# Decoder layer with a routed last stage: engine lists reordered at the step boundaries and in the last step

## The chip, the cores and the metric

The kernel runs on one core of a Trainium2 chip. The metric is the device time of one execution in microseconds, median of the runs shown.

## The reference

Three residual blocks over x of shape (4, 1024, 256), float32, each followed by a layer normalisation:

```python
x = _layernorm(x + gated_conv_scan(x))        # sigmoid gate, 5-tap conv, scan h = a*h + u, W_out, its own layernorm
x = _layernorm(x + slot_gru(x, ctx))          # 3 iterations, per batch: slots = x (1024 rows), context of 64 rows:
    #   attn = softmax over slots of (rmsnorm(slots) @ Wq.T) @ k.T; attn /= sum over context; updates = attn @ v
    #   r, z = sigmoid(...); n = tanh(xn + r * hn); slots = (1 - z) * n + z * slots   (six 256x256 products)
x = _layernorm(x + expert_w[argmax(x @ gate_w.T)] @ x)   # 8 experts, each token goes through one of them
```

## The kernel before, in words

**Stages.** The first block fills the first 113 us. The second takes most of the rest: three iterations over two pairs of batches are six *steps*, k = 0 to 5 (`LAST` = 5). A step is eight *units* (k, q), q = 0 to 7, each 24 matmuls of 128x512 on TensorE (`unit`, L1394): in the order R, HN, XN, Z, each with `hidden` products (six matmuls on the slots, split into `slots_hi` and `slots_lo` for precision) and `update` products (two on `at`, the attention, likewise split). XN is update products alone. The products of a unit land in PSUM banks that the other engines read: ScalarE makes r (`r_gate`), n (`n_gate`) and z (`z_gate`); VectorE makes r*hn (`hidden_part`, L1797), adds xn (`input_part`, L1804), both together being `candidate(k, q)`, and mixes in `settle(k, q)` (`mix`, L1822 and L1824; after every second unit the cast to `slots_hi`, L1829); GpSimd makes slots minus n (`difference`, L1015) and `slots_lo` (L1028).

**Attention between the steps.** While step k runs, the attention of step k+1 is made, since two steps in a row are of different batch pairs: `mean_squares` on TensorE (L1322, fed by `ss_low`, L1755 on VectorE), then `scores` and `sums` (TensorE), exponentials and the `normaliser` on ScalarE (Ln, then Exp), and last on VectorE `attention(k+1)`: the product `sc` (L1779, 128x1024) and, for each half h of the pair, a cast to `at` (L1788) and the difference for its low part (L1790). ScalarE loads a new function table before Ln and before sigmoid or tanh.

**What sets the order.** Each engine runs its own list, written out by hand, and waits on semaphores. There is no scheduler: a call moved in the list of an engine moves the work.

**The last step.** Between the units of step 5 stand 32 *token tiles* (`token_tile`, L1353, 4 matmuls on 128 tokens: gate scores and transposed rows), each followed by `score` (VectorE, L1846) and `row`, `row_square` (ScalarE, L767, L774). Tokens are routed in *groups* of tiles: `choose(g)` and `destinations(g)` on VectorE with `ranks(g)` on TensorE between, `side(g)`, and then GpSimd sends every tile's rows to their place in a buffer in device memory, sorted by expert (`send_row`, L1043, an indirect DMA per tile). Before, there are six groups of 8, 8, 4, 4, 4, 4 tiles. `add_ident` (L1906, VectorE) adds twice the identity to the expert weights once they are loaded; that carries the residual.

**Sorted tiles.** The sorted rows come back through SyncE's queue as 39 tiles (`gather`, three a group, TG = 3). Each goes through `turn` (TensorE transpose, L1454), `copy_turned` (ScalarE, L781), `expert` (TensorE, L1481, 4 matmuls), `statistics` (VectorE, L1982), `variance`, `inverse` (ScalarE), `offset` (VectorE, L2009), `normalise` (ScalarE, L797) and `send_out` (GpSimd, L1051, an indirect DMA). The first `NSOON` = 12 tiles are full and can be worked on when only the first `SOON` = 3 groups (20 token tiles) have been sent: `soon_table` says where they lie. The other `NLAST` = 27 need all groups, and two tables on VectorE, `last_counts` and `last_places`, and SyncE waits for them (`base_set`).

```python
for g in range(SOON):
    sp.wait_ge(row_out[g], 16 * GROUPS[g][1])     # L488
...
for g, (t0, n) in enumerate(GROUPS):              # L1122
    for t in range(t0, t0 + n):
        send_row(t, g)
```

## Time and profile before

| | us |
|---|---|
| median of 3 runs | 638.34 (637.24 to 638.39) |
| the profiled execution | 638.83 |
| its span in the profile | 637.1 |
| TensorE busy | 546.8 (86%) |
| VectorE busy | 457.4 (72%) |
| ScalarE busy | 373.3 (59%) |
| GpSimd busy | 253.5 (40%) |
| mean granted TensorE clock | 0.922 |

The span is the time between the first and the last instruction; the run time adds 1.7 us around it. Busy times are of one core, and the engines overlap. All starts below are in microseconds from the span's start. A matmul row's end is modelled, so rows of TensorE can overlap by a little.

### The profile page before, as it was taken

How to read it: one execution, taken by the hardware profiler on the slowest of the kernel's cores; microseconds unless marked ns; L12 is line 12 of the kernel's file. 1: busy time of each engine (PE TensorE's matmuls, PEld its weight loads, DVE VectorE, ACT ScalarE, POOL GpSimd, SP SyncE). 2: the span in 40 equal slices, each digit the busy share in tenths (PEclk: the TensorE clock that was granted, in tenths of full speed). 3: DMA queues.
4: the chain of work that ended last, by engine and by line, in shares of the span. 5: the costliest groups of instructions: out<-in, count | busy, mean ns of one | idle time of the engine just before them, and what ended most of it. 6: DMA issues, size and time to landing. Idle time of an engine off the chain costs nothing.

```text
span 637.1 us, 7357 instructions
## 1 busy us (share of the span) xinstructions
PE 546.8 (86%) x2158; PEld 402.8 (63%) x2158; DVE 457.4 (72%) x806; ACT 373.3 (59%) x661; POOL 253.5 (40%) x239
## 2 busy tenths in 40 slices
PE   6999897597799979997997999799989886858781
PEld 3474536265578857876785788578878764636560
DVE  3999899985894995799489758964756579653431
ACT  4558195865665846584666668475756544634542
POOL 1032302021042564456454744543443462554453
PEclk9999897679899989998999999899999997878776
DMA  8921003010110000000000000020110724145421
GB/s 296 329 82 66 1 0 132 0 68 0 67 66 1 1 1 1 1 0 1 1 0 1 1 1 1 1 66 24 42 51 26 254 102 125 69 127 141 121 77 34
DMA packets 23896, 37.88 MB, mean 59 GB/s; under 512 B 3246, under 2 KB 15663, under 8 KB 23601
## 3 DMA queue, kind: packets, MB, share of 16 engines
q1 hardware_dynamic: 20448, 28.98, 14.5%
q0 software_dynamic: 3408, 8.43, 3.7%
q8 instruction: 18, 0.29, 0.2%
q14 instruction: 22, 0.17, 0.1%
HBM read 23.60 MB, written 14.72 MB: 60 GB/s over the span
## 4 chain that ended last, share of the span: by engine, by line
PE 46%; DVE 19%; issue 10%; ACT 8%; another core or an unknown queue 1%; POOL 0%; ACTq 0%; DVEq 0%; POOLq 0%
PE psum L1409 25%; PE psum L1481 7%; PE psum L1334 4%; DVE slots_full L1824 2%; DVE gru L1822 2%; DVE gru L1797 2%; PE psum L1454 2%; DVE at L1788 2%; PE psum L1158 2%; DVE sc L1779 2%; PE psum L1379 2%; DVE at L1790 2%; DVE ss_part L1755 1%; PE psum L1228 1%; PE psum L1247 1%
## 5 line engine op out<-in xcount | busy, mean ns | idle before, releaser
L1409 PE MATMUL psum<-slots_hi,w_hh 128*128 128x512 f32 x576 | 189.3, 411 | 15.3 <-DVE gru L1797 12.0
L1409 PEld LDWEIGHTS psum<-slots_hi,w_hh 128*128 128x128 f32 x576 | 109.4, 194 | 42.8 <-DVE gru L1797 13.7
L1015 POOL TENSOR_TENSOR gru<-slots_full,gru 128x512 f32<-128x512 f32 x43 | 67.8, 1576 | 161.7 <-ACT gru L744 161.6
L1409 PE MATMUL psum<-slots_lo,w_hh 128*128 128x512 f32 x288 | 116.7, 405 | 0.0
L1409 PE MATMUL psum<-at,v_ih_pair 128*128 128x512 f32 x288 | 92.9, 404 | 2.1 <-DVE at L1790 2.1
L1797 DVE SCALAR_TENSOR_TENSOR gru<-psum,vec,gru 128x512 f32<-128x512 f32 x48 | 35.9, 748 | 46.7 <-PE psum L1409 40.1
L1481 PE MATMUL psum<-slots_full,w_tile 128*128 x156 | 54.2, 482 | 14.7 <-issue 8.5
L1409 PEld LDWEIGHTS psum<-at,v_ih_pair 128*128 128x128 f32 x288 | 54.8, 193 | 17.1 <-DVE at L1790 3.9
L744 ACT ACTIVATE gru<-gru,vec 128x512 f32<-128x512 f32 x48 | 34.7, 723 | 52.3 <-DVE gru L1804 51.5
L1409 PEld LDWEIGHTS psum<-slots_lo,w_hh 128*128 128x128 f32 x288 | 55.8, 194 | 13.4
L1145 PE MATMUL psum<-early_hi,w_in 128*128 128x512 f32 x128 | 57.6, 608 | 5.1 <-DMA early_hi<-in_xT 4.9
L1028 POOL TENSOR_TENSOR slots_lo<-slots_full,slots_hi 128x512 fp32r<-128x512 f32 x32 | 52.3, 1634 | 0.6 <-DVE slots_hi L1829 0.6
L1051 POOL DMA_INDIRECT out<-out_tile,out_index x39 | 38.2, 979 | 34.1 <-ACT out_tile L797 23.6
L738 ACT ACTIVATE gru<-psum,brz 128x512 f32<-128x512 f32 x48 | 32.8, 682 | 30.4 <-PE psum L1409 29.7
L1481 PEld LDWEIGHTS psum<-slots_full,w_tile 128*128 128x128 f32 x156 | 33.6, 238 | 24.8 <-issue 20.5
L1043 POOL DMA_INDIRECT sorted_rows<-row_block,dest x32 | 32.9, 1028 | 36.8 <-DVE dest L1882 24.9
L1145 PEld LDWEIGHTS psum<-early_hi,w_in 128*128 128x128 f32 x128 | 24.7, 195 | 35.6 <-issue 33.8
L1824 DVE TENSOR_TENSOR slots_full<-gru 128x512 f32<-128x512 f32 x48 | 38.1, 795 | 1.7
L1982 DVE BATCH_NORM_STATS2 st<-psum 128x6 f32<-128x256 f32 x39 | 16.7, 428 | 28.8 <-PE psum L1481 19.1
L781 ACT ACTIVATE w_tile<-psum 128x256 f32<-128x256 f32 x39 | 14.9, 384 | 37.6 <-PE psum L1454 20.6
L1822 DVE TENSOR_TENSOR gru<-gru 128x512 f32<-128x512 f32 x48 | 35.2, 733 | 0.2
L751 ACT ACTIVATE gru<-psum,brz 128x512 f32<-128x512 f32 x48 | 32.7, 682 | 4.1 <-PE psum L1409 3.1
(250 smaller groups left out, 1015.3 us busy)
## 6 DMA issues: line engine op xcount, KB each, us to landing
gathered<-sorted_rows SPq DMA_DIRECT2D x39, 129.0 KB, 1.9
x_scratch<-slots_full SPq DMA_DIRECT2D x8, 512.0 KB, 3.0
x_block<-x_scratch SPq DMA_DIRECT2D x8, 512.0 KB
early_hi<-in_xT SPq DMA_DIRECT2D x3, 1024.0 KB, 5.7
x_tm<-in_x SPq DMA_DIRECT2D x4, 512.0 KB, 6.9
slots_full<-in_expertT SPq DMA_DIRECT2D x1, 2048.0 KB, 11.1
sorted_rows<-gru SPq DMA_DIRECT2D x1, 1032.0 KB, 12.1
early_hi<-in_xT SPq DMA_DIRECT2D x2, 512.0 KB, 4.3
```

What stands on the lines that cost most here:

```text
L738: act.activation(X(u), psum[:, R_B + u % 2, :], ACT.Sigmoid, bias=brz[:, c, 0:1]).then_inc(r_act, 1)
L744: act.activation(X(u), X(u), ACT.Tanh, bias=col(c, V_BIH + 2)).then_inc(n_act, 1)
L1015: pool.tensor_tensor(DF(u), full[:, c, seq(k, h), blk(j)], X(u), ALU.subtract).then_inc(d_pool, 1)
L1028: last = pool.tensor_tensor(slots[1][:, c, b, blk(j)], full[:, c, b, blk(j)], slots[0][:, c, b, blk(j)].bitcast(F32), ALU.subtract)
L1043: pool.indirect_dma_start(rows[:], bass.IndirectOffsetOnAxis(dest[:, n:n + 1], 0), rowb[:, row_slot(n), :], None, bounds_check=E * REGION - 1,
L1051: pool.indirect_dma_start(out[:], bass.IndirectOffsetOnAxis(oidx[:, g % 4, t:t + 1], 0), og[:, i % (4 * TG), :], None, bounds_check=TOK - ...
L1145: last = pe.matmul(psum[:, bank + j, :], wi[:, k, at_col:at_col + P], xF[b % 2][:, k, cols_of(j)], start=k == 0, stop=k == C - 1)
L1409: last = pe.matmul(psum[:, bank, :], w, d, start=start and i == 0, stop=stop and i == len(pairs) - 1)
L1481: last = pe.matmul(expert_out(i), wT[:, i % TG, c, :], ew[:, c, bass.ds(off, D)], start=c == 0, stop=c == C - 1)
L1797: dve.scalar_tensor_tensor(out=X(u), in0=psum[:, HN_B, :], scalar=col(c, V_BHH + 2), in1=X(u), op0=ALU.add, op1=ALU.mult).then_inc(t_dve, 1)
L1822: dve.tensor_tensor(Z(u), Z(u), DF(u), ALU.mult).then_inc(e_dve, 1)
L1824: dve.tensor_tensor(full[:, c, seq(k, h), blk(j)], X(u), Z(u), ALU.add).then_inc(s_dve, 1)
```

## The change

1. **Between steps, VectorE.** `attention` keeps its product; the two halves' cast and difference become `spread_attention(f, h)`. Before: `candidate(k, 6)`, `settle(k, 5)`, product, both halves, `candidate(k, 7)`, `settle(k, 6)`. Now: `candidate(k, 6)`, product, half 0, `settle(k, 5)`, `candidate(k, 7)`, `settle(k, 6)`, half 1.
2. **ScalarE tables.** After the Exp of `rms` and of `normaliser` the table for sigmoid and tanh is named at once, so that nine loads fall away (46 to 37 in its list).
3. **Last step, TensorE.** Token tiles come about three sooner (tiles 0 and 1 already inside unit (4, 7)), and there are five groups, of 8, 8, 8, 4, 4 tiles. `ranks(0)` to `ranks(2)` stand inside units 2, 4 and 5, `ranks(3)` after unit 7, and tiles 28 to 31 between the first turns instead of behind the third expert product.
4. **15 sorted tiles ahead of the rest.** `NSOON` is 15 and `NLAST` 24; since group 2 has 8 tiles, 24 token tiles have to be sent before the first gather. `last_counts` moves before `offset(0)` and `last_places` before `offset(1)` on VectorE.
5. **`add_ident` goes to GpSimd** (a 128x1024 addition each), ahead of the row sends of group 2 and of group 3; `mean_f` is rewritten to twice the identity for it.
6. **Smaller ones.** The last `add_block` on VectorE is split in two halves; `out_index` waits for `turn_ev`; the last group of three sorted tiles is finished as two and one; the waits for the output DMAs at the end go from GpSimd to SyncE; gathers of tiles 12 to 14 wait for turned tiles.

```diff
-        GROUPS = ((0, NT), (NT, NT), (2 * NT, TJ), (2 * NT + TJ, TJ), (3 * NT, TJ), (3 * NT + TJ, TJ))
+        GROUPS = ((0, NT), (NT, NT), (2 * NT, NT), (3 * NT, TJ), (3 * NT + TJ, TJ))
...
-        NSOON = 4 * TG
+        NSOON = 5 * TG
...
                     act.activation(inv[:], inv[:], ACT.Exp, scale=-1.0).then_inc(d_rd, 1)
+                    act.preload_act_table_set("sigmoid_and_others")
...
+                def add_ident(c):
+                    pool.wait_ge(ew_in, 16)
+                    part_c = ew[:, c].rearrange("p (e d) -> p e d", d=D)[:, :, c * P:(c + 1) * P]
+                    eye = mean_f[:].rearrange("p (a n) -> p a n", a=1).broadcast_to([P, E, P])
+                    pool.wait_ge(two_set, 1)
+                    pool.tensor_tensor(part_c, part_c, eye, ALU.add).then_inc(ew_id, 1)
...
                 for g, (t0, n) in enumerate(GROUPS):
+                    if g == 2:
+                        add_ident(0)
+                    if g == 3:
+                        add_ident(1)
                     for t in range(t0, t0 + n):
                         send_row(t, g)
...
                     candidate(k, 6)
+                    attention(k + 1)
+                    spread_attention(k + 1, 0)
                     settle(k, 5)
-                    attention(k + 1)
+                    if not later:
+                        gate_centre()
                     candidate(k, 7)
-                    settle(k, 6)
+                    if later:
+                        settle(k, 6)
+                    spread_attention(k + 1, 1)
```

VectorE's list at the end of a step, before, from the cast that ends `settle(k, 5)` on (L1779 the product, L1788 and L1790 a half's cast and difference, L1797 and L1804 `candidate(k, 7)`, L1822 and L1824 `settle(k, 6)`, L1755 `ss_low`):

```order
L1829 CAST slots_hi<-slots_full 128x2x512
L1779 SCALAR_TENSOR_TENSOR sc<-sc,small,inv 128x1024
L1788 CAST at<-sc 64x1024
L1790 TENSOR_TENSOR at<-sc,at 64x1024
L1788 CAST at<-sc 64x1024
L1790 TENSOR_TENSOR at<-sc,at 64x1024
L1797 SCALAR_TENSOR_TENSOR gru<-psum,vec,gru 128x512
L1804 TENSOR_TENSOR gru<-psum,gru 128x512
L1822 TENSOR_TENSOR gru<-gru 128x512
L1824 TENSOR_TENSOR slots_full<-gru 128x512
L1755 TENSOR_TENSOR ss_part<-ss_block,ss_part 128x512
```

And now, from the cast of the first half on (L1822 is now a half's cast and L1824 its difference, L1856, L1858 and L1863 are `settle`, L1831 and L1838 `candidate(k, 7)`, L1788 `ss_low`):

```order
L1822 CAST at<-sc 64x1024
L1824 TENSOR_TENSOR at<-sc,at 64x1024
L1856 TENSOR_TENSOR gru<-gru 128x512
L1858 TENSOR_TENSOR slots_full<-gru 128x512
L1863 CAST slots_hi<-slots_full 128x2x512
L1831 SCALAR_TENSOR_TENSOR gru<-psum,vec,gru 128x512
L1838 TENSOR_TENSOR gru<-psum,gru 128x512
L1856 TENSOR_TENSOR gru<-gru 128x512
L1858 TENSOR_TENSOR slots_full<-gru 128x512
L1822 CAST at<-sc 64x1024
L1824 TENSOR_TENSOR at<-sc,at 64x1024
L1788 TENSOR_TENSOR ss_part<-ss_block,ss_part 128x512
```

The product and the first half have moved ahead of `settle(k, 5)`, the second half behind `settle(k, 6)`; the set of operations is the same.

TensorE's list before, from the last token tile that stands in the last step (`hot`, `cum` are `ranks(3)`, `gathered` a turn, `w_tile` an expert product):

```order
L1379 MATMUL psum<-eye_and_gate,slots_full 128x137 x2
L1391 MATMUL psum<-hot_1,tri 128x32
L1392 MATMUL psum<-cum_1,ones_f 128x32
L1454 MATMUL psum<-ident,gathered 128x128 x4
L1479 TENSOR_LOAD soon_off
L1479 ISA x2
L1481 ISA
L1481 MATMUL psum<-slots_full,w_tile 128x256
L1481 ISA
L1481 MATMUL psum<-slots_full,w_tile 128x256
```

And now, from `ranks(3)` on:

```order
L1416 MATMUL psum<-hot_1,tri 128x32
L1417 MATMUL psum<-cum_1,ones_f 128x32
L1482 MATMUL psum<-ident,gathered 128x128 x2
L1401 MATMUL psum<-eye_and_gate,slots_full 128x137 x4
L1482 MATMUL psum<-ident,gathered 128x128 x2
L1401 MATMUL psum<-eye_and_gate,slots_full 128x137 x4
L1506 TENSOR_LOAD soon_off
L1506 ISA x2
L1508 ISA
L1508 MATMUL psum<-slots_full,w_tile 128x256
L1508 ISA
L1508 MATMUL psum<-slots_full,w_tile 128x256
```

Tiles 28 to 31 have come in among the first two turns.

GpSimd's list before, from the last `difference` calls (L1015) and `add_x1` (L1037) to the sends:

```order
L1037 TENSOR_TENSOR slots_full<-slots_full,x_block 128x2x512
L1015 TENSOR_TENSOR gru<-slots_full,gru 128x512 x2
L1037 TENSOR_TENSOR slots_full<-slots_full,x_block 128x2x512
L1015 TENSOR_TENSOR gru<-slots_full,gru 128x512
L1037 TENSOR_TENSOR slots_full<-slots_full,x_block 128x2x512
L1015 TENSOR_TENSOR gru<-slots_full,gru 128x512 x2
L1043 DMA sorted_rows<-row_block,dest 33920x258 x32
L1051 DMA out<-out_tile,out_index 4096x256 x39
```

And now (L1031 `difference`, L1053 `add_x1`, L1143 the rewriting of `mean_f`, L1061 `add_ident`):

```order
L1053 TENSOR_TENSOR slots_full<-slots_full,x_block 128x2x512
L1031 TENSOR_TENSOR gru<-slots_full,gru 128x512 x2
L1053 TENSOR_TENSOR slots_full<-slots_full,x_block 128x2x512 x2
L1143 TENSOR_SCALAR mean_f<-ident 128x128
L1031 TENSOR_TENSOR gru<-slots_full,gru 128x512 x3
L1066 DMA sorted_rows<-row_block,dest 33920x258 x16
L1061 TENSOR_TENSOR slots_full<-slots_full,mean_f 128x8x128
L1066 DMA sorted_rows<-row_block,dest 33920x258 x8
L1061 TENSOR_TENSOR slots_full<-slots_full,mean_f 128x8x128
L1066 DMA sorted_rows<-row_block,dest 33920x258 x8
L1074 DMA out<-out_tile,out_index 4096x256 x39
```

The two additions stand ahead of the sends of group 2 and of group 3, in the queue that also issues the DMAs.

## Rows read from the trace of the kernel before

**Rows 1.** The page: the chain that ended last, its share of the span by engine.

```profile
PE 46%; DVE 19%; issue 10%; ACT 8%; another core or an unknown queue 1%; POOL 0%; ACTq 0%; DVEq 0%; POOLq 0%
```

**Rows 2.** Windows (start:end, length, busy per engine, granted clock, DMA share, GB/s), step 3.

```profile
304.30:331.40 27.10, 27.09 (x116) 21.90 (x117) 15.82 (x22) 19.12 (x22) 10.29 (x8) 1.00 0.00 1
331.40:363.30 31.90, 28.40 (x114) 21.89 (x113) 30.46 (x30) 19.11 (x25) 20.65 (x14) 0.95 0.00 1
```

**Rows 3.** TensorE's waits, 200 to 480 us (total, times, longest).

```profile
PE psum L1409 <- DVE gru L1797: 12.0, 4, 3.0
PE psum L1409 <- DVE at L1790: 2.1, 4, 0.9
```

**Rows 4.** TensorE in order of time (start, us) at the boundary 2 to 3.

```profile
349.74 1.22 PE L1409 MATMUL psum<-slots_hi,w_hh 128*128 128x512 f32 x2 [3.00 <-DVE gru L1797]
...
363.29 0.73 PE L1322 MATMUL psum<-ss_part,mean_half 128*128 128x512 f32 x2
```

**Rows 5.** VectorE in order of time at the same boundary.

```profile
340.68 2.31 DVE L1779 SCALAR_TENSOR_TENSOR sc<-sc,small,inv 128x1024 f32<-128x1024 f32 x1
...
343.75 2.20 DVE L1790 TENSOR_TENSOR at<-sc,at 64x1024 fp32r<-64x1024 f32 x1
...
348.93 0.75 DVE L1797 SCALAR_TENSOR_TENSOR gru<-psum,vec,gru 128x512 f32<-128x512 f32 x1
...
361.45 1.78 DVE L1755 TENSOR_TENSOR ss_part<-ss_block,ss_part 128x512 fp32r<-128x512 f32 x1
```

**Rows 6.** VectorE at the boundary 4 to 5, the same operations.

```profile
457.18 1.28 DVE L1779 SCALAR_TENSOR_TENSOR sc<-sc,small,inv 128x1024 f32<-128x1024 f32 x1
...
459.22 1.22 DVE L1790 TENSOR_TENSOR at<-sc,at 64x1024 fp32r<-64x1024 f32 x1
```

**Rows 7.** ScalarE at the boundary 2 to 3.

```profile
340.33 1.28 ACT L751 ACT_TABLE_LOAD   x1
...
342.21 1.04 ACT L759 ACTIVATE sq_block<-slots_full 128x1024 f32<-128x1024 f32 x1
343.16 0.68 ACT L738 ACTIVATE gru<-psum,brz 128x512 f32<-128x512 f32 x1
```

**Rows 8.** TensorE in the last part, from the first sorted tile.

```profile
534.65 0.67 PE L1454 MATMUL psum<-ident,gathered 128*128 128x128 f32 x2
...
538.74 2.07 PE L1481 MATMUL psum<-slots_full,w_tile 128*128 x4 [2.26 <-issue]
...
544.95 2.21 PE L1379 MATMUL psum<-eye_and_gate,slots_full 128*128 128x137 f32 x16
...
549.12 0.39 PE L1390 MATMUL psum<-cum,ones_f 128*128 128x8 f32 x2 [0.50 <-DVE hot L1864]
...
565.85 0.69 PE L1454 MATMUL psum<-ident,gathered 128*128 128x128 f32 x2 [3.65 <-issue]
566.71 3.77 PE L1481 MATMUL psum<-slots_full,w_tile 128*128 x8 [0.17 <-issue]
...
574.60 1.73 PE L1481 MATMUL psum<-slots_full,w_tile 128*128 x4 [3.27 <-issue]
...
579.91 1.13 PE L1481 MATMUL psum<-slots_full,w_tile 128*128 x4
```

**Rows 9.** GpSimd: row sends in order of time; its 128x1024 addition by line.

```profile
507.82 0.97 POOL L1043 DMA_INDIRECT sorted_rows<-row_block,dest  x1 [6.61 <-DVE dest L1882]
...
556.39 0.98 POOL L1043 DMA_INDIRECT sorted_rows<-row_block,dest  x1 [0.30 <-issue]
...
L1037 POOL TENSOR_TENSOR slots_full<-slots_full,x_block 128x1024 f32<-128x1024 f32 x4 | 9.6, 2395 | 0.0
```

**Rows 10.** SyncE's queue: its waits, 520 to 640 us.

```profile
SPq L488 <- DMA sorted_rows<-row_block,dest: 1.9, 1, 1.9
```

**Rows 11.** VectorE: first and last instruction of the two tables (24 in all).

```profile
555.39 0.16 DVE L1944 TENSOR_SCALAR gru<-soon_first 128x8 f32<-128x8 f32 x1
...
561.52 0.24 DVE L1978 TENSOR_SCALAR gru<-gru,i_col 128x27 int32<-128x27 f32 x1
```

More of the change, by code:

```diff
@@ L2133, in _ @@
+                score(26)
+                hidden_part(LAST, 7)
+                score(27)
+                input_part(LAST, 7)
+                choose(3)
+                settle(LAST, 7)
+                add_half(1)
+                destinations(3)
                 side(3)
-                destinations(3)
-                score(26)
-                score(27)
+                for n in range(28, 32):
+                    score(n)
                 choose(4)
-                settle(LAST, 7)
-                add_block(7)
+                statistics(0)
```

396 lines of the change are left out of this document (211 added, 185 removed).

## Prediction

> **What bounds the kernel now.** I read the chain of waits first: TensorE carries 46% of it, VectorE 19% [rows 1]. So neither engine bounds all of the time, and the question is where they change places. I then cut one step (59 us) into two windows [rows 2]. From 304.30 to 331.40 TensorE is busy 27.09 of 27.10 us, and VectorE 15.82: TensorE bounds. From 331.40 to 363.30, around the boundary to the next step, TensorE is busy 28.40 of 31.90 us and VectorE 30.46: there VectorE bounds, with 1.4 us of idle time in 32. TensorE's waits in the steps say the same: four waits for `hidden_part` (L1797) make 12.0 us, 3.0 at each boundary, and four for the low half of the attention make 2.1 [rows 3]. In order of time, TensorE stands 3.00 us until 349.74, because VectorE first finishes product, halves and their casts (from 340.68) and comes to `hidden_part` of unit 7 at 348.93 [rows 4, 5]. The window's last matmul, the mean squares at 363.29, starts when VectorE's `ss_low` ends (361.45 + 1.78 = 363.23) [rows 4, 5]: VectorE's list, not TensorE's, sets when the boundary is over.
>
> In the last part sorted tiles go one after another through all engines. What to see in [rows 8]: the first expert product starts at 538.74, the twelve early tiles end at 566.71 + 3.77 = 570.48, with 3.65 us of waiting before the turn at 565.85; then comes a gap up to 574.60, where the first late tile starts.
>
> **The change, part by part.**
>
> *The boundaries 0-1 to 3-4 (four).* In the new order the product can begin at about 338.8, right behind `candidate(k, 6)`, since it no longer waits for `settle(k, 5)` (some 1.9 us ahead of 340.68, which are `mix` and the cast). Uncontended it takes 1.28 [rows 6] (2.31 in [rows 5]); half 0 follows with a cast and 1.22 to 2.20 [rows 5, 6] and is done by about 343, where TensorE wants it at about 345.5: the wait of 2.1 / 4 = 0.5 goes. `settle(k, 5)` then ends at about 345.2. Here a new wait comes. ScalarE's squares need that settle, and `r_gate` of unit 7 stands behind them: before it ran at 343.16 [rows 7]; now squares (1.04) and gate (0.68) follow the settled slots of about 344.4, which gives 346.1, and VectorE idles some 0.95 us. `hidden_part` of unit 7 ends at about 346.9 instead of 349.7, so TensorE's wait of 3.0 becomes about 1.0. That looks like 2.5 us a boundary. But the operations on VectorE are the same, only in another order, and the next unit's `hidden_part` now stands behind half 1 (about 1.9 us): it ends about where it did, TensorE runs into it, and `ss_low` is as late as before. Over the window VectorE can give back only its idle 1.4 us [rows 2] and what it loses to operations that take longer beside GpSimd's (1.03 for the product, 0.98 for a difference [rows 5, 6], and one cast, not shown, of about the same size): 3.0 together. Against it stand the new idle 0.95 and, at worst, contention for the operations that were free of it. **I take 0 for each**, as nearest to the balance of VectorE's busy time (30.46 of 31.90), with bounds of -3 and +2 us: -12 and +8 for four.
>
> *Table loads.* Nine loads of 1.28 us fall away (the row at 340.33 is one [rows 7]), 11.5 us of ScalarE time. ScalarE waits on VectorE and TensorE around every one of them; `z_gate` comes 1.3 us sooner and its result is wanted later. Value 0; its cover is VectorE's queue, and were that gone, each boundary's load would be worth at most 1.3.
>
> *Boundary 4-5.* Tiles 0 and 1 inside unit (4, 7) wait for `gate_centre`, tile 2 for score and row of tile 0. These waits replace one of the same size. Three tiles more are done when step 5's unit 1 starts, so I carry about 0.65 us of delay, which is hidden behind the next term.
>
> *Up to the first sorted tile.* What decides there is GpSimd's queue: 24 tiles are sent before the first gather, where it was 20. Group 1 began at 507.82 [rows 9], and since `ranks(1)` comes inside unit 4, I put it 2.2 us sooner, at 505.6. A send costs 1.28 us in a row (0.97 and 0.30 between). Then: 8 sends 10.2, `add_ident(0)` 2.4 (the 128x1024 addition by its row [rows 9]), 8 sends 10.2, landing and reading the place about 3.0 (SyncE's wait for it was 1.9 [rows 10]), gather and turn 2.5: 533.9, against 534.65 [rows 8]. With tiles 28 and 29 in the gap behind it I put the first expert product at 537.5 against 538.74: **-1.2**.
>
> *Early tiles.* Before, twelve took 570.48 - 538.74 = 31.7 us. Out of this go tiles 28 to 31 (2.2, the row at 544.95), the ranks of the sixth group (from 549.12, three pairs of small matmuls, some 0.9) and the wait of 3.65, whose chain runs over the tables on VectorE (555.39 to 561.8 [rows 11]): they delayed statistics of tiles 6 to 8, and now stand two groups of tiles sooner, where TensorE goes slower anyway. In come about 1.0 us of waiting, since `offset(0)` and `offset(1)` stand behind the tables. 31.7 - 2.2 - 0.9 - 3.65 + 1.0 = 26.0: the twelfth ends at 563.5. Tiles 12 to 14 follow at the pace of the late ones, (579.91 - 574.60) / 3 = 1.77 [rows 8], until 568.8; the gap at the switch stays (574.60 - 570.48 = 4.1): the first late tile, number 15, at 572.9. Before, it ran at 579.91. **-7.0**. Bounds: -1 (the tables stop the early tiles for their full 6.4 us) and -11 (the gap goes too, since the last send, which ended at 557.4 [rows 9], will end near 549).
>
> *The end.* The last tiles go out as fast as GpSimd issues them, and the split of the last group changes only when the first two are ready: 0. Moving the final waits from one queue to another: 0.
>
> Sum: 638.8 (the profiled execution) - 7.0 = 631.8. That execution is 0.5 us above the median of 638.34, so against the median **631.3**, with the likeliest case's own range of 627 to 635.5.
>
> **Rivals.**
>
> *B, the boundaries gain too.* If the pieces of attention fall where GpSimd is idle, three contended operations a boundary become free: 4 x 3.0 = 12 us more, 619.3. For it: the product begins at 338.8, before GpSimd has the `difference` of unit 6 to do, and VectorE is the bound. Against it: GpSimd's operations start when VectorE's and ScalarE's results come, so they move along.
>
> *C, the additions on GpSimd cost their full time.* They stand between sends that are on the way to the first turn and to the last send, 2.4 us each [rows 9]; if VectorE's routing operations, which read two operands from SBUF, wait for them too, `destinations(3)` and `destinations(4)` are late by as much: 2 x 2.4 = 4.8 off the gain, 636.1. For it: the product on VectorE took 2.31 instead of 1.28 us beside an operation of GpSimd [rows 5, 6]. The Trainium skill, "SBUF — State Buffer", section "Who interferes with whom", says that a VectorE instruction with two SBUF inputs and a GpSimd instruction that reads SBUF lock each other out of a shared port for the whole instruction; it speaks against this part of the change. By that rule the loser would stand still for up to a whole operation, and the trace agrees in direction, with 1.03 us lost where GpSimd's operations take 1.5 or more. Against C: GpSimd stands idle before the sends of group 3, so the second addition may cost nothing.
>
> *D, slower: the new wait of VectorE at each boundary.* Its place is `r_gate(k, 7)` behind the squares. VectorE idles 0.95 us, and where the product falls together with `difference` all the same and one more operation does, 1.03 more are lost; TensorE is behind VectorE for the rest of the window, so both are paid in full: 4 x 2.0 = 8 us, with 0.65 at the last boundary, against the gain of 7.0: 640.0. It decides from 1.7 us a boundary on. For it: 30.46 of 31.90 us busy. Against it: in three of the five operations contention is there already, and it can only move.
>
> *E, nothing.* The sorted tiles are bound by another thing than I think and all gains are waited away: 638.3.
>
> **Chances.** My forecast 0.50, B 0.18, C 0.15, D 0.13, E 0.04. A measurement of this kernel can tell 0.2% (1.3 us) from no change. A, B and C lie below 637.1; a part of C and of A's tail reaches into the band. Faster 0.80, same 0.07, slower 0.13. The range takes in B and most of D: 619 to 640.
>
> **What would show it right or wrong.** Right: at each boundary TensorE's wait of 3.0 splits into two shorter ones, behind `hidden_part` of unit 7 and of the next step's unit 0, and the step stays at 59.0 us; the first turn stands within 1 us of 533.9; no wait over 2 us in front of turn 11; the first late tile at about 573. Wrong: steps of 56 us (B), or of 61 (D, with `r_gate` as what VectorE waits for); a first turn after 536 with GpSimd's additions ahead of it (C); or a wait of 3 us or more behind `last_counts` or `last_places`, which would mean that the tables' price was set too low.

## The result, and the profile after

| | before | after |
|---|---|---|
| median, us | 637.79 (636.31 to 638.39, 4 runs) | 644.64 (644.07 to 644.92, 4 runs) |
| ratio | | 1.011, 95% interval 1.0089 to 1.013 |
| span of the profiled execution | 637.1 | 643.1 |
| mean granted TensorE clock | 0.922 | 0.939 |

The change makes the kernel slower by 1.1%, 6.9 us. The prediction, 631.3 with a range of 619 to 640, is wrong in its sign.

The same places in both traces say where the time went. "Unit (k, q)" is the start of VectorE's `hidden_part` (L1797 before, L1831 now).

| start of | before, us | after, us | difference |
|---|---|---|---|
| the last mean squares of step 1 | 245.30 | 245.14 | -0.2 |
| the same, step 2 | 304.31 | 307.12 | +2.8 |
| the same, step 3 | 363.29 | 369.12 | +5.8 |
| the same, step 4 | 423.27 | 431.11 | +7.8 |
| unit (4, 7) | 463.44 | 472.19 | +8.8 |
| unit (5, 0) | 468.62 | 483.79 | +15.2 |
| unit (5, 7) | 528.94 | 545.09 | +16.2 |
| first expert product | 538.74 | 555.34 | +16.6 |
| sorted tile 15 | 579.91 | 590.37 | +10.5 |
| last expert product | 621.86 | 629.21 | +7.4 |
| end of the span | 637.1 | 643.1 | +6.0 |

So three things happened: the boundaries between steps cost about 9 us up to unit (4, 7), the boundary 4-5 another 6.4 (three more token tiles stand in it, 1.4 us of matmuls at the pace of 0.47 a tile), and the last part, from the first expert product on, gave 10.6 back. Step 5 between them adds 1.4.

The page after, its engines and its chain:

```profile
PE 545.1 (85%) x2154; PEld 401.1 (62%) x2154; DVE 460.6 (72%) x795; ACT 360.6 (56%) x654; POOL 254.6 (40%) x242
...
PE 39%; DVE 23%; issue 12%; ACT 10%; another core or an unknown queue 1%; POOL 0%; POOLq 0%; DVEq 0%; ACTq 0%
```

VectorE carries 23% of the chain where it had 19% [rows 1], ScalarE 10% where it had 8%, TensorE 39% where it had 46%.

**A step.** The window of one whole step, between the same matmuls (columns as in [rows 2]):

```profile
307.10:369.10 62.00, 57.06 (x228) 44.90 (x228) 47.54 (x51) 35.23 (x44) 29.31 (x20) 0.94 0.00 1
```

62.0 us for 228 matmuls, where before it was 27.1 + 31.9 = 59.0. TensorE's waits in the steps, as in [rows 3]:

```profile
PE psum L1434 <- DVE gru L1831: 11.5, 8, 2.0
PE psum L1349 <- DVE ss_part L1788: 10.3, 4, 3.7
```

The four waits of 3.0 us behind `hidden_part` have become eight of 11.5 us in all, the half's wait (2.1) is gone, and four have come, 10.3 us in all, before the last mean squares of each step (L1349), where VectorE's `ss_low` (`ss_part`) is late. Before, there was one such wait in this stretch, of 1.3 us. In order of time at the boundary 2-3, as in [rows 4]:

```profile
351.19 0.73 PE L1434 MATMUL psum<-slots_hi,w_hh 128*128 128x512 f32 x2 [0.74 <-DVE gru L1831]
...
359.05 1.01 PE L1434 MATMUL psum<-slots_hi,w_hh 128*128 128x512 f32 x2 [1.99 <-DVE gru L1831]
...
369.12 0.87 PE L1349 MATMUL psum<-ss_part,mean_half 128*128 128x512 f32 x2 [2.21 <-DVE ss_part L1788]
```

The prediction had the first wait at 1.0 (it is 0.74) and one at unit 0 of the next step (1.99). It had not carried on to the third, 2.21 at the mean squares. VectorE at the same boundary, as in [rows 5]:

```profile
343.00 1.27 DVE L1812 SCALAR_TENSOR_TENSOR sc<-sc,small,inv 128x1024 f32<-128x1024 f32 x1
...
345.03 2.20 DVE L1824 TENSOR_TENSOR at<-sc,at 64x1024 fp32r<-64x1024 f32 x1
...
350.38 0.75 DVE L1831 SCALAR_TENSOR_TENSOR gru<-psum,vec,gru 128x512 f32<-128x512 f32 x1 [0.97 <-ACT gru L752]
...
351.78 1.16 DVE L1856 TENSOR_TENSOR gru<-gru 128x512 f32<-128x512 f32 x1
352.97 1.67 DVE L1858 TENSOR_TENSOR slots_full<-gru 128x512 f32<-128x512 f32 x1
354.67 1.68 DVE L1822 CAST at<-sc 64x1024 fp32r<-64x1024 f32 x1
...
358.25 0.74 DVE L1831 SCALAR_TENSOR_TENSOR gru<-psum,vec,gru 128x512 f32<-128x512 f32 x1
...
364.14 1.56 DVE L1856 TENSOR_TENSOR gru<-gru 128x512 f32<-128x512 f32 x1
365.73 1.67 DVE L1858 TENSOR_TENSOR slots_full<-gru 128x512 f32<-128x512 f32 x1
367.32 1.75 DVE L1788 TENSOR_TENSOR ss_part<-ss_block,ss_part 128x512 fp32r<-128x512 f32 x1
```

What to see here: the product takes 1.27 instead of 2.31, as hoped. The new idle time before `hidden_part` of unit 7 is 0.97, behind ScalarE's `r_gate`. But the difference of half 0 still takes 2.20; then `mix` of unit 6 takes 1.16 and 1.67, where both halves of it took 0.7 before, the cast of half 1 takes 1.68 (1.66 before), and `mix` of unit (3, 1) 1.56 and 1.67. All of them ran beside an operation of GpSimd. Before, the same two `mix` operations of unit 6 were these:

```profile
350.32 0.68 DVE L1822 TENSOR_TENSOR gru<-gru 128x512 f32<-128x512 f32 x1
351.04 0.69 DVE L1824 TENSOR_TENSOR slots_full<-gru 128x512 f32<-128x512 f32 x1
```

From the end of `candidate(2, 6)` to the end of the last `ss_low`, VectorE took 24.5 us (338.71 to 363.23) and takes 26.0 (343.08 to 369.07). Off it went 1.0 for the product, 1.1 for one of the two `ss_low` additions (1.77 before, 0.69 now) and an idle time of 0.8 ahead of unit (3, 1); onto it came 3.2 for `mix` and the new idle 0.97. ScalarE's two lines say why `r_gate` was late:

```profile
348.71 1.06 ACT L773 ACTIVATE sq_block<-slots_full 128x1024 f32<-128x1024 f32 x1 [3.46 <-DVE slots_full L1858]
349.68 0.67 ACT L752 ACTIVATE gru<-psum,brz 128x512 f32<-128x512 f32 x1
```

The squares wait for the settled slots (to 348.71, where [rows 7] had them at 342.21), and `r_gate` of unit 7 follows at 349.68.

The whole run says the same of VectorE by line (columns: name, shapes, count, busy us, mean ns, idle before it). Before, the two operations of `mix` and the product:

```profile
L1824 DVE TENSOR_TENSOR slots_full<-gru 128x512 f32<-128x512 f32 x48 | 38.1, 795 | 1.7
...
L1822 DVE TENSOR_TENSOR gru<-gru 128x512 f32<-128x512 f32 x48 | 35.2, 733 | 0.2
...
L1779 DVE SCALAR_TENSOR_TENSOR sc<-sc,small,inv 128x1024 f32<-128x1024 f32 x5 | 10.5, 2107 | 0.0
```

And after:

```profile
L1858 DVE TENSOR_TENSOR slots_full<-gru 128x512 f32<-128x512 f32 x48 | 47.0, 978 | 1.6
L1856 DVE TENSOR_TENSOR gru<-gru 128x512 f32<-128x512 f32 x48 | 42.1, 876 | 2.9 <-ACT gru L765 2.2
...
L1812 DVE SCALAR_TENSOR_TENSOR sc<-sc,small,inv 128x1024 f32<-128x1024 f32 x5 | 6.4, 1277 | 1.3 <-ACT inv L744 1.3
```

`mix` has grown from 73.3 to 89.1 us with the same 96 instructions; the product has shrunk from 10.5 to 6.4. The `ss_low` additions fell by 4.4 and the casts of the halves by 0.9, so VectorE works 6.4 us longer for the same work. In these lines the reorder put more on some operations than it took off others.

### The profile page after: what moved, and what is told of

Its sections match the earlier page's. It is cut to its first block, busy times and chain, and to the rows that moved or that the text cites. A ratio compares the mean times of both kernels' runs of the same rounds, so it can differ in the third digit from the quotient of the medians.

```text
span 643.1 us, 7343 instructions
## 1 busy us (share of the span) xinstructions
PE 545.1 (85%) x2154; PEld 401.1 (62%) x2154; DVE 460.6 (72%) x795; ACT 360.6 (56%) x654; POOL 254.6 (40%) x242
## 4 chain that ended last, share of the span: by engine, by line
PE 39%; DVE 23%; issue 12%; ACT 10%; another core or an unknown queue 1%; POOL 0%; POOLq 0%; DVEq 0%; ACTq 0%
PE psum L1434 19%; PE psum L1508 5%; DVE slots_full L1858 5%; DVE gru L1856 4%; PE psum L1361 3%; DVE gru L1831 2%; PE psum L1401 2%; DVE ss_part L1788 2%; DVE at L1822 2%; ACT gru L752 2%; PE psum L1185 2%; PE psum L1482 1%; ACT out_tile L814 1%; PE psum L1255 1%
## 5 line engine op out<-in xcount | busy, mean ns | idle before, releaser
L1434 PE MATMUL psum<-slots_hi,w_hh 128*128 128x512 f32 x576 | 191.2, 414 | 14.8 <-DVE gru L1831 11.5
L1434 PEld LDWEIGHTS psum<-slots_hi,w_hh 128*128 128x128 f32 x576 | 110.1, 196 | 44.2 <-DVE gru L1831 15.2
L1031 POOL TENSOR_TENSOR gru<-slots_full,gru 128x512 f32<-128x512 f32 x43 | 66.4, 1544 | 175.8 <-ACT gru L758 175.4
L1831 DVE SCALAR_TENSOR_TENSOR gru<-psum,vec,gru 128x512 f32<-128x512 f32 x48 | 35.9, 748 | 49.5 <-PE psum L1434 37.9
L1508 PE MATMUL psum<-slots_full,w_tile 128*128 x156 | 49.2, 444 | 13.4 <-ACT w_tile L795 8.0
L752 ACT ACTIVATE gru<-psum,brz 128x512 f32<-128x512 f32 x48 | 32.7, 681 | 44.3 <-PE psum L1434 42.2
L1044 POOL TENSOR_TENSOR slots_lo<-slots_full,slots_hi 128x512 fp32r<-128x512 f32 x32 | 48.4, 1512 | 0.6 <-DVE slots_hi L1863 0.6
L1858 DVE TENSOR_TENSOR slots_full<-gru 128x512 f32<-128x512 f32 x48 | 47.0, 978 | 1.6
L1172 PEld LDWEIGHTS psum<-early_hi,w_in 128*128 128x128 f32 x128 | 25.2, 199 | 36.7 <-issue 35.4
L1508 PEld LDWEIGHTS psum<-slots_full,w_tile 128*128 128x128 f32 x156 | 30.5, 217 | 22.9 <-issue 19.5
L1856 DVE TENSOR_TENSOR gru<-gru 128x512 f32<-128x512 f32 x48 | 42.1, 876 | 2.9 <-ACT gru L765 2.2
L1838 DVE TENSOR_TENSOR gru<-psum,gru 128x512 f32<-128x512 f32 x48 | 33.2, 692 | 1.8
L1038 POOL TENSOR_TENSOR ss_block<-sq_block 128x512 f32<-128x512 f32 x16 | 22.2, 1386 | 29.5 <-ACT sq_block L773 29.4
## 6 DMA issues: line engine op xcount, KB each, us to landing
sorted_rows<-gru SPq DMA_DIRECT2D x1, 1032.0 KB, 11.5
```

What stands on the lines that cost most here:

```text
L752: act.activation(X(u), psum[:, R_B + u % 2, :], ACT.Sigmoid, bias=brz[:, c, 0:1]).then_inc(r_act, 1)
L1031: pool.tensor_tensor(DF(u), full[:, c, seq(k, h), blk(j)], X(u), ALU.subtract).then_inc(d_pool, 1)
L1044: last = pool.tensor_tensor(slots[1][:, c, b, blk(j)], full[:, c, b, blk(j)], slots[0][:, c, b, blk(j)].bitcast(F32), ALU.subtract)
L1172: last = pe.matmul(psum[:, bank + j, :], wi[:, k, at_col:at_col + P], xF[b % 2][:, k, cols_of(j)], start=k == 0, stop=k == C - 1)
L1434: last = pe.matmul(psum[:, bank, :], w, d, start=start and i == 0, stop=stop and i == len(pairs) - 1)
L1508: last = pe.matmul(expert_out(i), wT[:, i % TG, c, :], ew[:, c, bass.ds(off, D)], start=c == 0, stop=c == C - 1)
```

## The experiments

The runs came in four series (e1 to e4; r1, r2, e5, e6; e7 to e10; x1 to x4), and the kernel before takes 620.5 us in the first two and about 638 in the others and in the first result: in its two traces (first result and r2) the starts agree within 1 us up to 465 us, and the last part is what differs. So every figure is read within its own series, against the kernel before in that series.

| run | median, us | before in its series | ratio, 95% interval |
|---|---|---|---|
| e1, old boundaries in the changed kernel | 622.99 | 620.67 | 1.0031 (1.0015 to 1.0048) |
| e2, new boundaries alone | 631.47 | 620.67 | 1.0186 (1.0169 to 1.0203) |
| e3, half 1 later | 616.31 | 620.67 | 0.9937 (0.992 to 0.9954) |
| e4, changed, no early tables | 633.12 | 620.67 | 1.0205 (1.0188 to 1.0222) |
| r1, changed again | 632.31 | 620.36 | 1.0183 (1.0151 to 1.0215) |
| r2, before again, one run | 622.76 | 620.36 | |
| e5, e1 and score(1) sooner | 620.54 | 620.36 | 0.9985 (0.9964 to 1.0006) |
| e6, e1 with 12 ahead | 622.14 | 620.36 | 1.0034 (1.0016 to 1.0052) |
| e7, gate ahead of squares | 641.4 | 637.89 | 1.0091 (1.0046 to 1.0135) |
| e8, early tables alone | 637.49 | 637.89 | 0.9999 (0.9978 to 1.002) |
| e9, e5 and identity on VectorE | 634.26 | 637.89 | 0.9939 (0.9918 to 0.9961) |
| e10, half 1 later and score(1) sooner | 631.39 | 637.89 | 0.9875 (0.9827 to 0.9922) |
| x1, changed, third time | 646.87 | 638.54 | 1.0156 (1.0089 to 1.0222) |
| x2, as e9 | 633.42 | 638.54 | 0.9947 (0.991 to 0.9984) |
| x3, as e5 | 632.92 | 638.54 | 0.993 (0.9901 to 0.9959) |
| x4, e10 and row(2) later | 628.28 | 638.54 | 0.9868 (0.9805 to 0.9932) |

**e1: the old boundaries in the changed kernel.**

```diff
                     candidate(k, 6)
+                    if later:
+                        settle(k, 5)
                     attention(k + 1)
                     spread_attention(k + 1, 0)
-                    settle(k, 5)
-                    if not later:
+                    if later:
+                        spread_attention(k + 1, 1)
+                    else:
+                        settle(k, 5)
                         gate_centre()
                     candidate(k, 7)
                     if later:
                         settle(k, 6)
-                    spread_attention(k + 1, 1)
+                    else:
+                        spread_attention(k + 1, 1)
```

`later` is true at the boundaries 1-2 to 3-4; the boundary 0-1 is written out ahead of the loop and has the same edit.

> The changed kernel with VectorE's list put back at the four boundaries 0-1 to 3-4 (settle, product, both halves, then candidate 7); all else as changed, and at the boundary 4-5 the settle only moves ahead of the product. Theory 1 (the reordered list costs about 2.6 us at each boundary through the idle time before hidden_part of unit 7 and more operations that run beside GpSimd's): 644.6 - 4 x 2.1 to 2.6 = 634 to 636. Theory 2 (the boundaries are neutral as forecast, and the loss sits in the last step: more tiles early, additions on GpSimd): 643 to 645.

The edit leaves the boundary 4-5 as it is in the changed kernel: there `settle(4, 5)` stays behind the product and half 0. What the expectation says of that boundary is wrong.

Measured: 622.99, and the changed kernel stood at 632.31 in the next series (r1) and, without its early tables, at 633.12 in this one. So the four boundaries are worth 9 to 10 us. The expectation's absolute numbers went by a before of 637.8; its difference of 8.4 to 10.4 holds.

**e2: the new boundaries alone, in the kernel before.**

```diff
                     candidate(k, 6)
+                    if later:
+                        attention(k + 1)
+                        spread_attention(k + 1, 0)
                     settle(k, 5)
-                    attention(k + 1)
+                    if not later:
+                        attention(k + 1)
+                        spread_attention(k + 1, 0)
+                        spread_attention(k + 1, 1)
                     candidate(k, 7)
                     settle(k, 6)
+                    if later:
+                        spread_attention(k + 1, 1)
```

> The kernel before with only the new order of VectorE's list at the boundaries 0-1 to 3-4. Theory 1: 637.8 + 8 to 10 = 646 to 648, with 61 to 62 us a step and a wait of TensorE for ss_part of about 2 us in each step. Theory 2: 637 to 639.

Measured: 631.47 against 620.67, +10.8 us, a little over the 8 to 10 expected. The window of a step:

```profile
306.90:368.90 62.00, 57.08 (x228) 44.91 (x228) 47.52 (x51) 38.01 (x46) 29.32 (x20) 0.94 0.00 1
```

62.0 us, VectorE busy 47.52, TensorE 57.08 at a granted clock of 0.94: the changed kernel's window within 0.02 us, though ScalarE still has its table loads (38.01 us here, 35.23 there). Theory 1 holds, from both sides, and the forecast of a neutral boundary falls.

**e3: half 1 later.** If VectorE's list bounds the boundary, work must be taken out of it, not turned round in it. TensorE wants half 1 only in unit 4 of the next step.

```diff
                     settle(k, 1)
+                    spread_attention(k, 1)
+                    dve.wait_ge(at_lo, 2 * k + 2)
                     tops(k + 1)
...
                     attention(k + 1)
+                    spread_attention(k + 1, 0)
+                    if not later:
+                        spread_attention(k + 1, 1)
                     candidate(k, 7)
```

As in e2, `attention` is first cut down to the product, so that the halves can be placed by themselves.

> The kernel before, with the second half of the attention (cast and difference) taken out of the boundary and put behind settle(k, 1) of the next step, where VectorE idles; TensorE needs that half only in unit 4. Theory 1 (VectorE's list bounds the boundary): each of four boundaries gives back 2 to 3 us: 626 to 630. Rival (TensorE or the chain through ScalarE bounds it): 636 to 639.

Measured: 616.31, 4.4 us under before: clear of the noise, and about half of the least expected (8 us). Its trace stands further ahead: the last mean squares of step 4 start at 414.23, 9.0 us before those of the kernel before. That trace is of the fastest of its four runs (614.54). One step of it and TensorE's waits:

```profile
298.70:355.70 57.00, 53.99 (x229) 42.64 (x229) 48.02 (x51) 37.87 (x46) 30.74 (x20) 1.00 0.00 1
```

```profile
PE psum L1322 <- DVE ss_part L1755: 10.3, 4, 2.6
```

57.0 us for this step and for the one before it, 58.6 for the one behind it; the waits for `hidden_part` are gone, and what is late next is the `ss_low` in front of the last mean squares, 2.6 us each. That is the wait that the new kernel has too.

**e4 and e8: the early tables, taken out and put in alone.**

```diff
                     act.activation(inv[:], inv[:], ACT.Exp, scale=-0.5).then_inc(rstd_done, 1)
-                    act.preload_act_table_set("sigmoid_and_others")
...
                     act.activation(inv[:], inv[:], ACT.Exp, scale=-1.0).then_inc(d_rd, 1)
-                    act.preload_act_table_set("sigmoid_and_others")
```

This is e4, in the changed kernel; e8 puts the same two lines into the kernel before.

> The changed kernel without the two early table loads, so that the nine loads before sigmoid come back (11.5 us of ScalarE time). If ScalarE is off the path: within 1 us of 644.6. Rival (z_gate of unit 6 and the normaliser's neighbours are on the path): 647 to 650.

> The kernel before with only the early table loads (nine loads fewer). Forecast: no change, within 1 us of the kernel before. Rival (z_gate of unit 6 comes 1.3 us sooner, so that squares, slots_lo and r_gate do, and operations fall apart otherwise): 1 to 4 us faster, or slower where more of VectorE's operations then meet GpSimd's.

Measured: e4 1.0205 of before, the changed kernel in the next series 1.0183, intervals that overlap; e8 0.9999 (0.9978 to 1.002). Taking 11.5 us of work from ScalarE changes nothing that can be measured (e8's interval is 0.2% to either side, 1.3 us).

**r1, r2 and x1: the two kernels again.**

> The changed kernel unaltered, so that the others of this series have it beside them on the same chip. If the four boundaries cost 10 us, as the first series says, and the early tables nothing: within 1 us of the kernel without early tables, 632 to 634, where the kernel before has 620.7. If the early tables were worth something: 630 or less.

> The kernel before unaltered, for its profile on this chip: the same starts up to about 470 us, and a last part that is shorter by about 15 us than in the first profile (620.7 against 637.8 us).

> The changed kernel unaltered on the chip of this series. 1.1 to 1.8% above the kernel before (its two ratios so far: 1.011 and 1.018).

Measured: the changed kernel is slower each time, by 1.1%, 1.8% and 1.6%. r2 took 622.76 in its one timed run, with a span of 621.0. In it the last part runs so (first expert product, first late tile):

```profile
536.23 2.07 PE L1481 MATMUL psum<-slots_full,w_tile 128*128 x4 [2.56 <-issue]
...
568.54 1.81 PE L1481 MATMUL psum<-slots_full,w_tile 128*128 x4 [4.01 <-ACT w_tile L781]
```

32.3 us between them and 52.5 from there to the end, where the first profile of before had 35.9 and 62.5 [rows 8].

**e5: score(1) sooner.** At the boundary 4-5 ScalarE of the changed kernel stands as follows (`row(1)`, then `z_gate` of unit (4, 7), then `r_gate` of unit (5, 0)):

```profile
480.22 0.47 ACT L781 ACTIVATE row_block<-psum,token_scores 128x256 f32<-128x256 f32 x1 [3.90 <-DVE token_scores L1880]
480.59 0.68 ACT L765 ACTIVATE gru<-psum,brz 128x512 f32<-128x512 f32 x1
...
483.08 0.67 ACT L752 ACTIVATE gru<-psum,brz 128x512 f32<-128x512 f32 x1
```

`row(1)` waits 3.90 us for a score, and both gates stand behind it. The score itself stood on VectorE behind `settle(4, 6)`, whose two operations took 1.55 and 2.75 beside two of GpSimd.

```diff
                         score(0)
+                        score(1)
                         settle(k, 6)
...
-                score(1)
                 score(2)
```

> The changed kernel with the old boundaries (as in e1_old_boundaries, 623.0), and score(1) moved on VectorE from behind settle(4, 6) to ahead of it. Theory (at the boundary 4-5 ScalarE has row(1) in front of z_gate of unit 7, and row(1) waits for a score that stands behind two long operations): r_gate of unit (5, 0) comes 3 to 4 us sooner, 619 to 621. Rival (GpSimd's sends or the extra tiles set the last step's end): 622 to 624.

Measured: 0.9985 of before, against 1.0031 for e1: 2.8 us for one moved reduction of 0.2 us. The traces have 1.9 of it at its place: `hidden_part` of unit (5, 0) follows that of (4, 7) by 9.7 us, where it is 11.6 in e1 and in the changed kernel, and 5.2 in the kernel before.

**e6: twelve tiles ahead.** `NSOON = 4 * TG` in e1.

> The changed kernel with the old boundaries and 12 sorted tiles ahead of the last ranks instead of 15 (27 late ones). Theory (three more early tiles move the gap at the switch to a later, then shorter, place): 1 to 3 us slower than 623.0. Rival (the gap waits for the last sends in both cases): the same within 0.5.

Measured: 1.0034 against 1.0031. The rival holds: the wait at the first late tile is there with both counts, and as long (3.77 here, 3.96 in e1):

```profile
568.17 1.13 PE L1508 MATMUL psum<-slots_full,w_tile 128*128 x4 [3.77 <-ACT w_tile L795]
```

So the fifteen sorted tiles, by themselves, gain nothing in these two series.

**e7: the gate ahead of the squares.**

```diff
                     z_gate(k, 6)
+                    r_gate(k, 7)
                     if later:
                         squares(k, 2)
-                    r_gate(k, 7)
```

> The changed kernel with ScalarE's r_gate of unit 7 put ahead of the squares at the boundaries 0-1 to 3-4, so that hidden_part no longer waits for it. It tells the idle time from the contention. If the idle 0.97 us is a loss of its own: 4 us faster than the changed kernel (which is 11.8 us above the kernel before on this chip), thus 7 to 9 us above before. If VectorE's contended operations only take the place of the idle time: 10.5 to 12 above before.

Measured: 1.0091 (1.0046 to 1.0135), 3.5 us over the kernel before, where 7 to 9 was expected if the idle time is a loss of its own. The changed kernel was not run in this series, and the interval is too wide to part 4 us from 1. The traces say more. From the matmuls with `mean_half` on `res` inside step 0 (L1247 of the kernel before, at 187.50) to unit (4, 6) the kernel before takes 266.9 us, the changed kernel 276.9 and e7 272.8. But of the 4.1 us between the last two, 3.1 are two stretches behind the last mean squares that ran at the full granted clock in e7 (35.05 and 35.10 us, where the changed kernel has 36.62 and 36.61), and one such stretch also ran at the full clock in the unaltered changed kernel (r1, 35.08). The four boundaries proper got 1.0 us shorter in all, though four idle times of 0.97 at the gate are gone. So in these traces `r_gate` behind the squares itself costs about 1 us; that the clock held because of its move is not shown. Two boundaries of e7 in order of time:

```profile
304.52 0.74 PE L1349 MATMUL psum<-ss_part,mean_half 128*128 128x512 f32 x2 [0.93 <-DVE ss_part L1788]
...
354.66 0.73 PE L1434 MATMUL psum<-slots_hi,w_hh 128*128 128x512 f32 x2 [2.73 <-DVE gru L1831]
...
364.72 0.73 PE L1349 MATMUL psum<-ss_part,mean_half 128*128 128x512 f32 x2 [2.19 <-DVE ss_part L1788]
```

The wait at unit 7 becomes one of 2.73 at unit 0 of the next step, and the wait at the mean squares is there again, 2.19 at the second of these boundaries and 0.93 at the first.

**e9 and x2: the identity on VectorE.** The two additions go back to VectorE, behind `add_block(6)` and behind the first `add_half`, in e5.

> e5_score_1_sooner with the two additions of the identity back on VectorE (1.21 us each), behind add_block(6) and behind the first half of the last add_block. If GpSimd's additions hold sends or VectorE (rival C): 1 to 4 us faster than e5 (which was 0.2 us above before). If they are hidden there: 0 to 2 us slower, since VectorE has 2.4 us more in the last step.

> As e9_identity_on_vector, now beside x3 on the same chip. If GpSimd's additions cost the last step: 1 to 4 us under x3. If they are hidden: 0 to 2 us above x3.

> As e5_score_1_sooner. Its difference to x1 is four boundaries (10 us by e1) and the score (2.5 us by e5): 11 to 13 us under x1, thus 2 to 4 us under the kernel before where that stands 8 to 10 under x1.

Measured: e9 0.9939, where e5 had 0.9985 in another series; that looked like the 1 to 4 us of rival C. But beside each other in one series x2 takes 633.42 and x3 632.92, no difference. GpSimd's additions (2.4 us each) are hidden, and rival C falls. x3 is 14.0 us under the changed kernel beside it (11 to 13 was expected) and 5.6 under the kernel before (2 to 4 expected): without the reordered boundaries and with one score moved, the rest of the change is a gain (0.993, 0.9901 to 0.9959). In the series of e5 that gain was not to be told from nothing.

**e10 and x4: what beats both.** e10 is the changed kernel with the boundaries as in e3 and the score as in e5. x4 also puts `row(2)` behind `r_gate(LAST, 0)` on ScalarE.

> The changed kernel with three edits: at the four boundaries the old order, but the second half of the attention put behind settle(k, 1) of the next step (as in e3_half_1_later, which gained 4.4 us on before), and score(1) sooner (as in e5, at before's time). If the two gains add up: 4 to 8 us under before. Rival (the last step's end is set by GpSimd's sends, so that an earlier start is waited away): within 2 us of before.

> e10_all_but_reorder with row(2) and its square behind r_gate(5, 0) on ScalarE instead of ahead. In the trace of e5 ScalarE waited 1.97 us for the score of tile 2 there, with r_gate, and VectorE's hidden_part, behind it. If that delay reaches the end of the last step: 1 to 2.5 us under e10 (0.9875 of the kernel before), 0.984 to 0.986. Rival (the tiles' rows bound the last step again): 0.987 to 0.989.

Measured: 0.9875 and 0.9868, the second just above the 0.984 to 0.986 that was expected; 628.28 against 638.54 for before and 646.87 for the changed kernel in the same series. What `row(2)` did: ScalarE in x3 (row 2), and then in x4 (`r_gate`, then row 2):

```profile
470.17 0.47 ACT L781 ACTIVATE row_block<-psum,token_scores 128x256 f32<-128x256 f32 x1 [1.98 <-DVE token_scores L1880]
```

```profile
463.12 0.69 ACT L752 ACTIVATE gru<-psum,brz 128x512 f32<-128x512 f32 x1 [0.65 <-PE psum L1435]
464.01 0.48 ACT L781 ACTIVATE row_block<-psum,token_scores 128x256 f32<-128x256 f32 x1 [0.20 <-DVE token_scores L1881]
```

The wait of 1.98 is gone from in front of the gate, but unit (5, 0) comes only 0.3 us sooner behind (4, 7): 9.4 us instead of 9.7. The end of the run didn't follow by as much as can be measured (0.0007 between two ratios whose intervals are 0.01 wide), so that edit is not shown to be worth anything.

## Why the prediction was wrong

**The boundaries: this is the step that failed.** "I take 0 for each", with bounds of -3 and +2; measured +2.5 each on average (10.0 us up to unit (4, 6) in the trace, 10.8 in e2). By the places of the trace, 3.8 of the 10.0 are VectorE's list at the boundaries, and 6.2 are TensorE's granted clock in the stretches behind them, a term that the prediction didn't have. Rival D had named the new idle time behind `r_gate`, 0.95 us forecast and 0.97 measured, with a chance of 0.13. Its sign was right and its price of 2.0 a boundary near the measured 2.5, but for other reasons than it gave: without that idle time (e7) the boundaries get only 1.0 us shorter in all. In VectorE's share two things went wrong.

- The balance of busy time was read as an upper bound on a gain, and then as evidence for "the same". Where an engine is busy 30.46 of 31.90 us, little else can give: I wrote 0.95 of new idle time down and took 0 all the same.
- Contention was counted for the operations that were moved, and the others were left at their durations. The product no longer loses its 1.03, but the `mix` operations behind it, which had run free of GpSimd, do not any more: their lines grew by 15.8 us over the run. The trace agrees with the Trainium skill, "SBUF — State Buffer", section "Who interferes with whom", that the pair of engines gets in each other's way where VectorE reads two operands from SBUF: such a `mix` operation took 0.69 and takes 1.67. But the lesson is that GpSimd's operations wait for results of VectorE and ScalarE, as the prediction had said against rival B, so they come along wherever a block is moved.

The larger share is TensorE's clock. One stretch behind the last mean squares, up to the next mean squares, before and now:

```profile
304.31:339.37 35.06, 35.06 (x151) 28.30 (x152) 23.66 (x30) 26.16 (x30) 15.36 (x11) 1.00 0.00 1
```

```profile
307.12:343.73 36.61, 36.61 (x150) 29.42 (x151) 23.69 (x29) 24.10 (x28) 14.43 (x10) 0.95 0.00 1
```

TensorE is busy for all of it in both, with the same matmuls, and now takes 1.55 us longer for them. The loss lies in the first 5 us, where the granted clock is 0.66 (15 matmuls from 307.10 to 312.10, 22 in the same length before); the rest is at 1.00. The kernel before has one such fall in a step, behind its wait of 3.0 (0.66 from 349.30 to 354.30). The new kernel has two: that one, later (0.72 from 357.10 to 362.10), and the one behind the mean squares. The four stretches in five traces, with the wait that stands in front of each:

| trace | waits before the last mean squares, steps 1 to 4, us | stretches behind them, us (granted clock) |
|---|---|---|
| before | 1.34, none, none, none | 35.09 (1.00), 35.06 (1.00), 35.05 (1.00), 31.14 (1.00) |
| after | 2.16, 2.19, 2.21, 3.73 | 36.62 (0.95), 36.61 (0.95), 36.63 (0.95), 32.64 (0.95) |
| r1, changed again | 2.20, 3.74, 2.21, 2.21 | 35.08 (1.00), 37.79 (0.92), 36.62 (0.95), 32.69 (0.95) |
| e7, gate first | 2.18, 0.93, 2.19, 2.19 | 35.05 (1.00), 35.10 (1.00), 36.62 (0.95), 32.69 (0.95) |
| e3, half 1 later | 2.56, 2.60, 2.55, 2.60 | 35.06 (1.00), 35.07 (1.00), 36.62 (0.95), 32.56 (0.95) |

The fourth stretch is shorter because it is taken to `hidden_part` of unit (4, 6). From before to after the four grew by 6.2 us, and the boundaries between them by 3.8 (the one from 339.37 to 363.29 took 23.9, from 343.73 to 369.12 it takes 25.4). Every lost stretch stands behind a wait for `ss_low`, but of fifteen waits of 2.16 us or more four were followed by a stretch at full clock: the wait's length alone doesn't decide, and what does is open.

**Tables: right.** Nothing, as forecast (e4, e8).

**The boundary 4-5: not sized.** "These waits replace one of the same size", +0.65. Between unit (4, 7) and unit (5, 0) it cost 6.4 us, 1.4 of them the three tiles. TensorE's own waits there (2.18 for the gate's centre, where it had 1.85, then 1.06 and 1.81) are small beside it. The prediction did not look at what stands behind the waiting instruction on ScalarE: `row(1)` waits 3.90, and behind it stand two gates. e5 takes 1.9 us out there and is worth 2.8 in its ratio; the rest was not tried apart.

**Up to the first sorted tile: a late start was left out.** I made GpSimd's queue the bound and had the first turn at 533.9. It came at 549.35, and waited only 0.60 for the gather: TensorE itself had come to `ranks(3)` at 548.12, so the two were about equally late. The sends, as in [rows 9], with the addition among them:

```profile
518.12 0.97 POOL L1066 DMA_INDIRECT sorted_rows<-row_block,dest  x1 [3.52 <-ACT row_block L781]
...
528.13 2.41 POOL L1061 TENSOR_TENSOR slots_full<-slots_full,mean_f 128x1024 f32<-128x1024 f32 x1
532.72 1.48 POOL L1066 DMA_INDIRECT sorted_rows<-row_block,dest  x1 [2.18 <-DVE row_block L1926]
...
543.03 1.22 POOL L1066 DMA_INDIRECT sorted_rows<-row_block,dest  x1 [0.30 <-issue]
```

Group 1's sends start at 518.12 instead of the forecast 505.6, 12.5 us late, since the units before them are 15 us late. From there to the first turn it takes 31.2 us where the sum had 28.3. The addition at 528.13 is not the reason: behind it GpSimd still waits 2.18 for VectorE, and 5.85 behind the second one. The sum treated the last step as if it began on time: a chain whose start is set by one engine and whose end by another was followed only from the second. A delay of 0.65 could hide behind that term; 15.2 could not.

**Early tiles and the switch: right in sum, in part by luck.** From `ranks(3)` to the first late tile, as in [rows 8]:

```profile
548.12 0.41 PE L1416 MATMUL psum<-hot,tri 128*128 128x32 f32 x2 [1.49 <-DVE cum L1905]
...
549.35 0.44 PE L1482 MATMUL psum<-ident,gathered 128*128 128x128 f32 x2 [0.60 <-DMA gathered<-sorted_rows]
551.10 2.19 PE L1401 MATMUL psum<-eye_and_gate,slots_full 128*128 128x137 f32 x8 [1.31 <-DVE slots_full L1941]
...
555.34 1.91 PE L1508 MATMUL psum<-slots_full,w_tile 128*128 x4
...
567.48 0.67 PE L1482 MATMUL psum<-ident,gathered 128*128 128x128 f32 x2 [1.87 <-ACT out_tile L814]
...
584.78 1.12 PE L1508 MATMUL psum<-slots_full,w_tile 128*128 x4 [0.23 <-issue]
...
590.37 1.12 PE L1508 MATMUL psum<-slots_full,w_tile 128*128 x4 [4.02 <-ACT w_tile L795]
```

From the first expert product to tile 15 the forecast had 35.4 us (537.5 to 572.9); it took 35.0, against 41.2 before. The wait of 3.65 before turn 11 is gone, and the gap at the switch is 584.78 + 1.12 to 590.37, 4.5 us, near the 4.1 carried over. But where about 1.0 of new waiting was forecast, turns wait 1.87 (567.48) and 2.25 (575.76). The twelve tiles took 26.5 us against 26.0 forecast all the same. In them TensorE was busy 20.1 us at a granted clock of 0.83, where it had been busy 24.7 at 0.77; the sum had 3.1 of these 4.6 us, for the work moved away, and the other 1.5, at the higher clock, made up for part of the waits. The credit is open as well: no run takes back alone the four token tiles and the set of ranks that no longer stand between the expert products. e6 shows that the count of 15 has no part in it in the series where it was tried. How the rest divides between tiles 28 to 31, the larger third group and the tables' place was not tried apart.

**The late tiles and the end.** From tile 15 to the last expert product it took 41.9 us at a granted clock of 0.84 and takes 38.8 at 0.91; of these 3.1 us, for which the prediction had nothing, 2.3 are shorter busy time of TensorE. Why the clock is higher was not looked for. From the last expert product to the end of the span it took 15.2 and takes 13.9. That is 1.3 where 0 was forecast; which of the split of the last group and the moved final waits it is was not tried.

**The sign.** -7.0 for the last part was, by the table, -10.6; +15 at the five boundaries was missing, and 1.4 in step 5.

## What to carry to other kernels

On an engine that is busy 95% of a stretch, an order can only be better by the idle time and the contention that it removes; write both lists out to the next place where another engine waits, and price each operation again, not the moved ones alone. Where such a change puts a new wait in front of a stretch that TensorE bounds, read the granted clock of that stretch as well: here it cost more than the waits at the boundary. The move that pays takes an operation out of that stretch: half 1 was wanted four units after it was made, and putting it behind the stretch gained (e3; x4 against x3, which differ in `row(2)` too), while a new order inside cost 1.9% (e2). Where a chain crosses engines, follow the delay in the start of the last stage before summing gains inside it, and look at what is queued behind a waiting instruction on its own engine.

## What was not expected of the hardware

- The kernel before takes 620.5 us in two series and 638 in the others, with starts that agree within 1 us up to 465 us. The record has the same chip number for the two series at 620.5 and for the last one at 638.5, which speaks against the chip as the reason. From the first expert product to the last it takes 83.1 us in the first trace and 69.5 in r2; TensorE is busy 65.0 and 57.4 of them, at granted clocks of 0.78 and 0.82 (first trace, up to the first late tile and behind it) against 0.87 and 0.95 (r2). The lower clock thus goes with about 7.6 of the 13.6 us. Why it was lower, and why stalls of 2.4 to 4 us come at other tiles, is open. A forecast of a few us in such a stage holds for one series at a time, and kernels of different series can't be compared by their absolute times.
- A VectorE operation of 0.69 us (128x512, two SBUF operands) that took 1.67 beside GpSimd lost 0.98, and one of the same shape took 2.75 at the boundary 4-5, where GpSimd's additions of 128x1024 stand: it lost three times its length. A cast of 0.69 us (64x1024), which reads one operand, took 1.68 beside GpSimd too.
- A wait of TensorE of about 2.2 us before the mean squares cost another 1.5 us of clock in most cases (2.19 at 307.12, after) and nothing in others (2.18 at 244.32, e7; 2.60 at 298.70, e3).
